# A cross-attention and FFN kernel with its setup work and first steps in another order

## The reference

```python
x = x + xattn(layernorm(x), ctx)
x = x + ffn(layernorm(x))
# xattn: 16 heads of 32
kv_dca = (y_dca @ Wkv_dca + bkv_dca)          # -> k_dca (normed per head), v_dca
q = ln(x @ Wq + bq)                           # per head, with gain and shift
kv = [y_main @ Wk + bk, y_main @ Wv + bv]     # reshaped to 16 heads of 2 * 32
k = ln(kv[..., :32]); v = kv[..., 32:]
ctx = attn(q, k, v) + attn(q, k_dca, v_dca)
out = ctx @ Wo + bo
# ffn: 8-bit fake quantisation of x, kernel, bias; relu; fake quantisation of the result
```

## Time and profile before

| | us |
|---|---|
| median of 3 runs | 431.06 |
| lowest, highest | 428.88, 436.38 |
| the profiled execution | 428.96 |
| its span | 427.2 |

### The profile page before, as it was taken

How to read it: one execution, slowest core, us unless ns; L and a number is a source line. 1 busy time by engine, 2 the same in 40 slices (tenths; PEclk the granted TensorE clock), 3 DMA queues, 4 the chain that set the end, 5 groups by cost and what they waited for, 6 DMA issues and landing times.

```text
span 427.2 us, 7677 instructions
## 1 busy us (share of the span) xinstructions
PE 336.6 (79%) x2383; PEld 266.1 (62%) x2383; DVE 323.7 (76%) x829; ACT 212.4 (50%) x389; POOL 185.0 (43%) x269
## 2 busy tenths in 40 slices
PE   1064845739797999999999999999898999978621
PEld 0022634428686868787877778787777777756510
DVE  1396292493977899999898999999898998876442
ACT  0134452234273756575756656665656575562311
POOL 8400131022252727373654546373736355372532
PEclk9998858988899999999999999999999999998965
DMA  7903008014143526362726345362717153460001
GB/s 261 359 29 113 1 1 214 0 37 113 64 117 97 149 68 173 92 164 94 193 69 170 108 131 149 90 176 90 187 63 190 62 150 101 102 162 12 25 25 49
DMA packets 32867, 47.53 MB, mean 111 GB/s; under 512 B 9272, under 2 KB 19772, under 8 KB 32828
## 3 DMA queue, kind: packets, MB, share of 16 engines
q1 hardware_dynamic: 31296, 45.64, 38.2%
q10 hardware_dynamic: 1532, 1.42, 1.1%
HBM read 33.93 MB, written 13.11 MB: 110 GB/s over the span
## 4 chain that ended last, share of the span: by engine, by line
PE 36%; DVE 21%; issue 13%; POOL 3%; ACT 1%; DMA 0%; DVEq 0%; POOLq 0%
PE bank L1079 13%; PE bank L1183 9%; DVE neg_max L897 3%; PE bank L1279 3%; PE bank L1152 3%; DVE wq_raw L956 2%; PE bank L1290 2%; DVE f_small L1028 1%; DVE wq_raw L1005 1%; DVE seg_out L910 1%; DVE q_lo L1024 1%; DVE finals L886 1%; DVE f_stat L994 1%; DVE fk_raw L989 1%; DVE cT_lo L921 1%
## 5 line engine op out<-in xcount | busy, mean ns | idle before, releaser
L441 POOL TENSOR_TENSOR k_lo<-wkv_raw,k_hi 128x448 f16<-128x448 f32 x16 | 16.7, 1045 | 133.8 <-issue 119.1
L1183 PE MATMUL bank<-v_aug,prob_store 128*128 128x66 f32 x512 | 67.3, 275 | 6.7 <-DVE seg_out L910 6.0
L1183 PEld LDWEIGHTS bank<-v_aug,prob_store 128*128 128x128 f32 x512 | 63.2, 191 | 10.2 <-issue 7.8
L612 ACT ACTIVATE prob_store<-bank,exp_scale 128x512 f32<-128x512 f32 x64 | 42.3, 686 | 35.1 <-PE bank L1164 34.4
L897 DVE TENSOR_REDUCE neg_max<-bank 128x4 f32<-128x448 f32 (+1 forms) x128 | 45.2, 416 | 9.9 <-PE bank L1152 9.7
L456 POOL TENSOR_TENSOR finals<-seg_out 128x128 f32<-128x128 f32 x64 | 31.1, 488 | 33.4 <-DVE seg_out L910 30.5
L623 ACT ACTIVATE wkv_raw<-bank,affine 128x448 f32<-128x448 f32 (+1 forms) x32 | 22.4, 748 | 44.3 <-PE bank L1217 43.9
L1163 PE MATMUL bank<-q_stack,k_stack 128*128 128x128 f16 x256 | 34.7, 223 | 1.4 <-ACT maxT L527 1.4
L1164 PE MATMUL bank<-maxT,sel 128*128 128x128 bf16 x256 | 34.5, 222 | 0.0
L1079 PE MATMUL bank<-wq_hi,xT_hi 128*128 128x512 f32 x64 | 30.8, 481 | 0.0
L929 DVE TENSOR_REDUCE qk_ss<-wkv_raw 112x16 f32<-112x512 f32 (+1 forms) x32 | 21.5, 677 | 11.9 <-ACT wkv_raw L680 11.9
(11 more groups left out here) (195 smaller groups left out, 924.6 us busy)
## 6 DMA issues: line engine op xcount, KB each, us to landing
k_stack<-stack_scratch SPq DMA_DIRECT2D x32, 256.0 KB, 4.0
q_stack<-stack_scratch SPq DMA_DIRECT2D x64, 128.0 KB, 4.1
x_in<-in_x SPq DMA_DIRECT2D x16, 256.0 KB, 3.2
out<-finals SPq DMA_DIRECT2D x16, 256.0 KB, 4.2
y_in<-in_ctx SPq DMA_DIRECT2D x16, 128.0 KB, 2.7
y_dcaT<-in_x SPq DMA_DIRECT2D x8, 256.0 KB, 3.4
stack_scratch<-k_hi SPq DMA_DIRECT2D x16, 128.0 KB, 1.7
stack_scratch<-k_lo SPq DMA_DIRECT2D x16, 128.0 KB, 1.7
```

The costliest lines, as they stand in the source:

```text
L612: s.activation(flat(probs[:, gr % 2]), bank[4 + gr % 2][:, :], ACT.Exp, scale=exp_scale[:, 0:1]).then_inc(probs_ready.sem, 1)
L1183: last = mm(bank[6 + gr % 2][:, VW * h:VW * (h + 1)], probs[:, gr % 2, h], v_aug[:, Bt.parity, HG * gr + h], start=True, stop=True)
```

## The change

The work is the same; what is done once is ordered anew, and the semaphores `whi_ready` and `wlo_ready`, which counted all weights, become one per weight. Step by step:

- SyncE's loads: tokens of batch 0, Wk, Wv, Wq, tokens of batch 1, Wo, FFN weights, `bias_split`, then the two bias rows. The wait for the DCA values and their store go into step -1, behind the stack loads of batch 0. In every step the load of `x_res` and the load of the DCA values move behind the stack loads, the latter from batch A to batch N.
- ScalarE's loads: biases and norms first, then the DCA tokens and wd_raw.
- GpSimd: `sel` is made ahead of step -2 and not before the first token statistics; the low parts of the values' weights (`low_values`) are GpSimd's; in step -1 the DCA low parts and columns come ahead of k_lo.
- VectorE: ahead of step -2 only the biases and the keys. In step -2, behind yT_lo, wd_raw, the norms and Wq (centred and split in two halves). The DCA scaling comes ahead of k_t and q_t in step -1; the FFN maxima, `setup_maxima` and wo_lo behind q_lo there. In step 0 `setup_output` comes ahead of the first `normalise`, `setup_ffn` behind the last.
- TensorE: the DCA projection in two halves, keys behind the K product of batch 0, values behind the Q product of batch 1, followed at once by `setup_output`, ahead of the first scores. The bias of K and Q is the last matmul of the product. The norm columns follow the Q product of batch 0.
- `dca_t` and `dca_sq` lie in spent tiles and not in wd_raw.

The core of the diff:

```diff
@@ SyncE
-            for i in range(2):
+            def tokens(i):
                 sp.dma_start(y_in[:, i], ctx[i]).then_inc(y_loaded.sems[i], 16)
                 sp.dma_start(x_in[:, i], x[i]).then_inc(x_loaded.sems[i], 16)
+
+            tokens(0)
+            for i in range(2):
                 load(wkv_in, wkv_raw[:, i], chunked((Wk, Wv)[i]))
             load(wq_in, wq_raw[:], chunked(Wq))
+            tokens(1)
             load(wo_in, wo_raw[:], chunked(Wo))
             load(fk_in, fk_raw[:], chunked(ffn_kernel))
-            load(fb_in, fb_row[:], row(ffn_bias))
-            load(bo_in, bo_row[:], row(bo))
...
+                    if N.first():
+                        sp.wait_ge(kvdca_ready.sem, 4)
+                    if N.has(2):
+                        sp.wait_ge(*xplus_ready.of(N.back(2)))
+                    sp.dma_start(x_res[N.parity], x[N.index()]).then_inc(xres_loaded.sem(N), 16)
+                    if N.first():
+                        sp.wait_ge(kvdca_copied.sem, 4)
+                        sp.dma_start(dca_scratch.rearrange("(j p) n -> p j n", p=P), kv_dca[:, :, 1]).then_inc(dca_stored.sem, 16)
+                        sp.wait_ge(dca_stored.sem, 16)
+                    if N.has(2):
+                        sp.wait_ge(*pv_ready.of(N.back(2)))
+                    sp.dma_start(v_aug[MAIN:P, N.parity, :, HD:2 * HD],
+                                 dca_rows[N.index()].rearrange("p (h d) -> p h d", d=HD)
+                                 ).then_inc(vdca_loaded.sem(N), 16)
@@ GpSimd
+            def low_values():
+                pool.wait_ge(wvhi_ready.sem, 2)
+                for n in range(2):
+                    g.tensor_tensor(value_half(wv_lo[:], n), value_heads(n), value_half(wv_hi[:].bitcast(FP32), n),
+                                    ALU.subtract).then_inc(wvlo_ready.sem, 1)
@@ ScalarE
-            run(act, step, {-2: setup_projections, -1: setup_heads, 0: setup_ffn})
+            run(act, step, {-2: setup_keys, -1: setup_heads})
@@ VectorE
+            def setup_keys():
                 setup_biases()
+                dve.wait_ge(wkv_in.sem, 16 * 2)
+                for n in range(2):
+                    centre(key_heads(n), head_mean[:, 1 + n, 0:YC, 0:H // 2], wkv_centred)
+                for n in range(2):
+                    low_keys(n)
+
+            def setup_queries():
+                dve.wait_ge(wd_in.sem, 16)
+                centre(wd_raw[:, :, 0].rearrange("p c (h d) -> p c h d", d=HD), head_mean[:, 0, 0:YC], wd_centred)
                 setup_norms()
                 dve.wait_ge(wq_in.sem, 16)
-                centre(wq_raw[:].rearrange("p c (h d) -> p c h d", d=HD), XC, head_mean[:, 3], wq_centred)
+                centre(wq_raw[:].rearrange("p c (h d) -> p c h d", d=HD), head_mean[:, 3], wq_centred, 2)
+                low_queries()
...
-            run(dve, step, {-2: setup_projections, -1: setup_squares, 0: setup_maxima})
+            run(dve, step, {-2: setup_keys, -1: setup_affine})
@@ TensorE
+            def setup_keys():
                 pe.wait_ge(ydcaT_copied.sem, 1)
                 pe.wait_ge(wd_centred.sem, 1)
                 for j in range(2):
+                    for c in range(YC):
+                        mm(bank[4 + j][:, :], y_dcaT[:, j, c, :], wd_raw[:, c, 0, :], start=c == 0, stop=False)
+                    mm(bank[4 + j][:, :], ones3[:], bias_split[:, 2], start=False, stop=True).then_inc(kvdca_ready.sem, 1)
+
+            def setup_values():
+                for j in range(2):
+                    if j:
+                        pe.wait_ge(*kn_ready.of(Batch(0)))
+                    for c in range(YC):
+                        last = mm(bank[7 - j][:, :], y_dcaT[:, j, c, :], wd_raw[:, c, 1, :], start=c == 0, stop=c == YC - 1)
                     last.then_inc(kvdca_ready.sem, 1)
...
                 if A is not None:
                     if A.first():
-                        pe.wait_ge(wlo_ready.sem, 4)
+                        pe.wait_ge(wklo_ready.sem, 2)
+                        pe.wait_ge(tiles_made.sem, 8)
+                        pe.wait_ge(bias_split_ready.sem, 48)
...
+                if N is not None and N.first():
+                    setup_values()
+                    setup_output()
...
-            run(pe, step, {-2: setup_projections, -1: setup_columns, 0: setup_output})
+            run(pe, step)
```

More of the change, by code:

```diff
@@ L457, in combine @@
                                     ALU.add).then_inc(ctx_ready.sem, 1)
+                if A is not None and A.first():
+                    low_values()
                 if D is not None:
@@ L464, in step @@
                 if N is not None:
-                    if N.has(1):
-                        dca_columns()
-                    low(k_lo, k_n, k_hi, kn_ready, khi_ready, k_put, klo_ready, MAIN)
                     if N.first():
@@ L476, in step @@
                         dca_columns()
+                    else:
+                        dca_columns()
+                    low(k_lo, k_n, k_hi, kn_ready, khi_ready, k_put, klo_ready, MAIN)
                 centred()
@@ L699, in step @@
                     s.activation(q_sq, q_raw[:, A.parity], ACT.Square).then_inc(qsq_ready.sem, 1)
+                if N is not None and N.first():
+                    setup_ffn()
                 if D is not None:
@@ L761, in low_weights @@
-            def low_weights(k, lo, hi, src):
-                dve.wait_ge(whi_ready.sem, k)
-                v.tensor_tensor(lo[:], src, hi[:].bitcast(FP32), ALU.subtract).then_inc(wlo_ready.sem, 1)
+                each = heads.shape[1] // parts
+                for part in range(parts):
+                    at = slice(each * part, each * (part + 1))
+                    v.tensor_tensor(heads[:, at], heads[:, at],
+                                    means[:, at].unsqueeze(3).to_broadcast([P, each, heads.shape[2], HD]),
+                                    ALU.subtract).then_inc(done.sem, 1)
@@ L1043, in step @@
                                     ).then_inc(ln2_steps.sem, 1)
+                if Bt is not None and Bt.first():
+                    setup_output()
                 if D is not None and D.has(1):
@@ L1073, in split_product @@
                 first = chunks[0] == 0
-                if bias is not None and first:
-                    mm(dst, ones3[:, 0:m], bias, start=True, stop=False)
-                    first = False
+                end = xT_h.shape[1] - 1
                 for c in chunks:
```

239 lines of the change are left out of this document (129 added, 110 removed).

## The result

The changed kernel takes 418.41 us (median of 4 runs, 414.91 to 425.40) beside 432.63 us for the kernel before on the same chip (428.88 to 436.38): a ratio of 0.966, 95% interval 0.960 to 0.972. It is faster by 3.4%. The forecast was 409, range 403 to 417: the sign was right, the size was not. Of the 22.6 us that the sum wanted from the span, 10.3 came (427.2 to 416.9).

The account below looks back on a forecast made before the run. Setup, some 55 us of the first 133.2, was taken as the loss, with TensorE 79% and VectorE 76% busy. Step 1's marker, 110.6 to 88.0, gave 22.6 off: 406.4, 408.5 on the median's footing, 409 with clock loss; range 403 to 417.

Parts of the forecast that it names:

- Biases by 8.3, both key halves by 13.3: Setup on VectorE: biases done by 8.3 us, centring both key halves and low parts ended at about 13.3.
- wd_raw at 18: First step: the DCA weight load, issued near 7.7 us, lands at 18, bounds 14 and 24.8.
- Rival (a): Setup loads gate more: DCA weights at 22 to 24.8, VectorE shifts by 4 to 6.8; 413 to 416 us, chance 0.15.
- bias_split 23.4, K 3.0: First step: bias_split lands 1.4 us earlier, at 23.4, then TensorE's K product takes 3.0 us at the lower clock level.
- Q 31.2 to 34.3: First step on TensorE: batch 0's Q product, ready from both sides at 31, runs from 31.2 to 34.3 us.
- rival (b): TensorE at the lower clock level: key half, DCA values, output bias cost 3.5 us more each; 412 to 419, chance 0.13.
- wv_lo on GpSimd, its low parts, the DCA columns: GpSimd: wv_lo ends at 33, ahead of V at 36; DCA columns end at 44.5, ahead of k_hi; no cost.
- Step -1, 25.3 us, and the 5.6 us of the output bias: Marker 37.4 to 62.7; the output bias in front of the first scores costs 5.6 us there.
- Step 0, 25.3 us: A steady step, 19.4, plus 6.4 of VectorE work, less 0.5 for missing C and D work; before 32.4 us.
- The bias matmul moved, 0: K and Q products: bias matmul last instead of first, same seven and thirteen matmuls, 0 us.
- SyncE's new order, 0 with bounds -2 and +4: Steady steps: x_res and DCA values behind the stacks should not hold q_stack; 0 us, bounds -2 and +4 for 13 steps.
- Rival (e): Loads directly behind q_stack share its DMA engines and delay every stack: 435 us or more at 2.0 us per step, chance 0.03.

Follow-up runs that it names:

- the second execution: The changed kernel run and profiled again unedited, beside the kernel before: 417.54 us, ratio 0.967.
- the early issue: Changed kernel with DCA tokens and wd_raw issued on ScalarE's queue ahead of the six norm loads: 411.63 us, 0.949 of the kernel before.
- the wait moved: Changed kernel with the result's store right behind the q_stack loads and a wait for this step's PV product in front of x_res: 413.63 us.
- both cured and the output bias late: Changed kernel with SyncE's old steady order, DCA tokens and wd_raw ahead of the norm loads, output bias behind the first scores: 407.02 us, ratio 0.939.

## Why the prediction was wrong

Point by point, by its own steps:

- **Biases by 8.3, both key halves by 13.3.** The biases began at 5.74, near the 6 of the sum. Their last cast took 2.39 us, two tiny operations on the key means 1.20 and 1.05, and the keys' low parts ended at 17.1. No cost: the next gate was later still.
- **wd_raw at 18: the step that failed, 23.55.** I had taken 7.7 for its issue and the 9.8 us of the earlier trace rows for its way. The issue came 1.4 us later and the way took 14.4 us. The later issue is not what cost: in the second execution it came at 8.35 and the load was there at 24.02. The way was mis-sized. The 9.8 us belonged to a load issued at 2.71, ahead of Wv, Wq, Wo, the FFN weights and the norm loads; now all these are issued ahead of it. I had granted the small norm packets 0.5 us, and ScalarE's queue moved 0.10 MB from 9 to 13 us. Rival (a) is this case, and it had 22 to 24.8; the early issue (ready by 17.25) shows that the place in the queue did it.
- **The Trainium skill at this step.** "DMA: Bandwidth & Descriptors", section "Issuing engines are not separate DMA queues", says that loads of different issuing engines interleave on the same engines. The longer way of wd_raw on ScalarE's queue (14.4 us), beside SyncE's weights, fits it. So does bias_split, for which I had gone against it: issued 5.8 us earlier than before (9.91, not 15.67), it was there no earlier (next point). But a load's place in time still counts: moved ahead by 5.1 us it was there at least 6.3 us sooner. From the other section of that page of the Trainium skill, "Queues, rings and completion order", turns by packet, I had wd_raw at 14; the row says 23.55. From 9 to 13 us the trace is near to such turns, 612 packets against 707, but they were small ones; from 13 to 23.5 it is not, 620 against 1439. The 14 counted wd_raw's bytes from the issue on, as if nothing stood ahead on its own queue.
- **bias_split 23.4, K 3.0.** K ran from 24.73 to 27.7, 3.0 us as summed. The 1.4 us by which bias_split was to land earlier did not come: 24.73 for the 24.82 of the earlier trace rows, and 26.14 in the second execution. It cost nothing here, since wd_raw held Q until later. Key half at the higher level from 27.74, 4.0 us for 4.5.
- **Q 31.2 to 34.3.** 36.56 to 41.9. Five of the 7.5 us are wd_raw's; some 2 are rival (b)'s mechanism at a place where (b) did not have it: not in the key half but in Q, behind 4.79 us of idle. I had priced the lateness of a load, and not the clock after the idle time that it makes. In the second execution it was the other way round: Q took 3.1 us, but the first four passes of the key half 3.33 and the output bias 6.36, for 1.88 and 3.67 in the profile of after. These are places that (b) had named.
- **wv_lo on GpSimd, its low parts, the DCA columns.** V was not held (43.40, right behind the columns). Right.
- **Step -1, 25.3 us, and the 5.6 us of the output bias.** The step took 26.7. Taking the bias away brought the first scores from 69.84 to 64.26, 5.6 us earlier. Of this 3.2 reached the marker of step 1.
- **Step 0, 25.3 us.** 24.1. Together with step -1 50.8 for 50.6. Right in this execution, and partly by luck: of the eight profiles whose setup work is that of the changed kernel, four have 50.3 to 50.8 here and four 53.5 to 55.6. So half of them lose 3 to 5 us more in these two steps; three of those four have the output bias at 6.24 to 6.36 us.
- **The bias matmul moved, 0.** No difference to be seen.
- **SyncE's new order, 0 with bounds -2 and +4: the second step that failed.** 4.6 us from step 1's marker to the end in one execution, 1.9 in the other, and 3 to 5.7 over the twelve intervals. With the old order back, or the wait moved, that stretch takes 315.3, 314.1 and 314.5 us, less than the 316.6 that I had taken from before, so the order costs more than the table of markers shows. "A load behind q_stack should not hold it" was the wrong inference; it came from one load behind another on one queue. The wait at which SyncE used to stand for the PV product was no nuisance but what kept 670 KB away from the q_stack loads. Rival (e) named the mechanism but asked for all stacks being slower; the medians are unchanged at 4.1 us, single loads are 1 to 2 us late. So (e)'s size was wrong too: about 0.3 us per step, not 2.

By the sum, 7.7 and 4.6 us of missed gain are the 12.3 us between the forecast's span and the one measured (10.8 and 1.9 us in the second execution), and about the 9.4 us between the times. With both cured and the output bias late the kernel is at 407.

What stays open: how far the first two gains overlap, why a late q_stack landing falls on some steps and not on others, and why the output bias is at the lower level in some executions and not in others.

## What to carry to other kernels

When a load is moved back in a queue, take neither its issue time nor its way to landing from its old place: the way grows with what now goes ahead of it, on its own queue and on others, and by packets as well as by bytes. Price the compute behind a late load at both levels if the engine idles before it. Before a wait is removed from a DMA queue, list what will now go out beside the transfer that the next product waits for; a median landing time will not show the harm, its maximum and the consumer's idle time will. And profile the same kernel twice before a loss is put down to one step.

## What the runs showed that I had not expected

- A norm load of 16 KB took 1.53 us to issue at two places in a row, others of the same form 0.44 to 0.52; the issue of x_res behind q_stack likewise took 1.73 once and 0.42 in the step before.
- Q behind 4.79 us of idle TensorE was granted 0.50, behind 1.12 us (the early load) and 2.33 us (the second execution) it was granted 1.00; the same 13 matmuls took 5.3, 3.1 and 3.1 us.
- Small operations on VectorE vary in the stretch of the setup loads: 128x16 elements in 1.20 us, the same form in 0.17 in another run. No run shows why.
- The output bias's eight fp32 matmuls took 3.67 us in one execution of the changed kernel and 6.36 in the other, at the same place, and steps -1 and 0 together 50.8 and 55.5.
